# Attention's product written transposed to two column halves, copied, transposed back; its normalization later

## What is computed

```
x = layernorm(x + edge_layer(x, adj, adj, b))          # layer 0, "edge"
x = layernorm(x + graph_attention(x, W, a, beta, adj)) # layer 1, "att" and "gat"
x = layernorm(x + (adj @ x) @ weight + bias)           # layer 2, "gcn"
q, k, v = x @ Wq + bq, x @ Wk + bk, x @ Wv + bv        # layer 3, 8 heads of 64
scores = q @ k.T / 8 + (0 where adj else -1e9)
x = layernorm(x + softmax(scores) @ v)                 # the change is in softmax(scores) @ v
```

## Time and profile before

| | |
|---|---|
| median of 3 runs | 2856.92 us (2856.85 to 2857.3) |
| the profiled execution | 2855.93 us |
| its span, first to last instruction | 2854.1 us |
| busy: TensorE, its loads, VectorE, ScalarE, GpSimd | 97%, 88%, 75%, 57%, 53% |
| mean granted TensorE clock | 0.990 |

### The profile page before, as it was taken

How to read it: one execution, slowest core, us unless ns; L and a number is a source line. 1 busy time by engine, 2 the same in 40 slices (tenths; PEclk the granted TensorE clock), 3 DMA queues, 4 the chain that set the end, 5 groups by cost and what they waited for, 6 DMA issues and landing times.

```text
span 2854.1 us, 59257 instructions
## 1 busy us (share of the span) xinstructions
PE 2773.0 (97%) x18569; PEld 2514.3 (88%) x18569; DVE 2151.3 (75%) x6805; ACT 1631.1 (57%) x4616; POOL 1507.2 (53%) x1808
## 2 busy tenths in 40 slices
PE   4899999999999999999999999999999999999996
PEld 3799998999999999999999999899999999999986
DVE  7777777777777777777777777777777777777763
ACT  3455656655555556556555555655555555556553
POOL 6555555545545555555555555555555555555541
PEclk9999999999999999999999999999999999999997
DMA  3000000000000000000000000000000000000000
GB/s 119 16 20 27 30 18 26 29 18 26 28 20 26 26 22 26 26 22 26 26 22 26 26 22 26 20 27 26 18 26 29 18 26 29 18 26 29 9 16 23
DMA packets 41471, 74.06 MB, mean 26 GB/s; under 512 B 5584, under 2 KB 5712, under 8 KB 41424
## 3 DMA queue, kind: packets, MB, share of 16 engines
q1 hardware_dynamic: 41424, 73.49, 7.9%
HBM read 39.92 MB, written 33.55 MB: 26 GB/s over the span
## 4 chain that ended last, share of the span: by engine, by line
PE 96%; DVE 1%; issue 1%; ACT 1%; DMA 0%; POOL 0%; ACTq 0%; SPq 0%; POOLq 0%; DVEq 0%
PE rot L812 22%; PE rot L814 22%; PE rot L813 22%; PE rot L912 9%; PE rot L920 4%; PE rot L869 4%; PE score L812 2%; PE score L813 2%; PE score L814 2%; PE rot L961 2%; PE rot L889 2%; PE rot L893 2%; PE att_bank L942 0%; PE s_bank L877 0%; DMA probs<-in_L_gnn_W 0%
## 5 line engine op out<-in xcount | busy, mean ns | idle before, releaser
L337 POOL TENSOR_TENSOR ve<-mv,eps_col 128x1 f32<-128x1 f32 (+1 forms) x448 | 95.2, 212 | 679.6 <-DVE mv L609 351.2
L359 POOL TENSOR_TENSOR x2b<-x,bias 128x512 f32<-128x512 f32 x128 | 216.4, 1690 | 448.5 <-DVE x L657 448.5
L812 PE MATMUL rot<-w_hi,y_hi 128*128 128x512 f32 x1024 | 426.5, 417 | 5.4 <-DVE y_lo L649 4.6
L814 PE MATMUL rot<-w_hi,y_lo 128*128 128x512 f32 x1024 | 404.4, 395 | 0.0
L813 PE MATMUL rot<-w_lo,y_hi 128*128 128x512 f32 x1024 | 402.8, 393 | 0.0
L437 ACT ACTIVATE k_hi<-rot,kb_col 64x256 fp32r<-64x256 f32 x512 | 240.5, 470 | 271.6 <-PE rot L814 266.7
L551 ACT ACTIVATE probs<-score,sc_nmax 128x128 f32<-128x128 f32 x1024 | 357.8, 371 | 11.4 <-DVE sc_nmax L773 11.4
L599 DVE SCALAR_TENSOR_TENSOR k_lo<-rot,kb_col,k_hi 64x256 fp32r<-64x256 f32 x512 | 247.5, 483 | 93.3 <-ACT k_hi L437 87.7
L912 PEld LDWEIGHTS rot<-v_sb,probs_t 128*128 128x128 f32 x2048 | 241.5, 194 | 69.8 <-issue 58.5
L812 PE MATMUL rot<-xt_hi,wk_hi 128*128 128x256 f32 x1024 | 299.8, 293 | 0.0
L599 DVE SCALAR_TENSOR_TENSOR q_lo<-rot,qb_col,q_hi 128x256 fp32r<-128x256 f32 x256 | 112.1, 479 | 239.9 <-ACT q_hi L437 239.9
(11 more groups left out here) (122 smaller groups left out, 8383.2 us busy)
## 6 DMA issues: line engine op xcount, KB each, us to landing
x_in<-in_x SPq DMA_DIRECT2D x128, 256.0 KB, 2.6
out_x<-x SPq DMA_DIRECT2D x128, 256.0 KB, 2.1
probs<-in_L_gnn_W SPq DMA_DIRECT2D x1, 1024.0 KB, 7.6
v_sb<-in_L_gnn_weight SPq DMA_DIRECT2D x1, 1024.0 KB, 7.1
probs<-in_L_gnn_Wv SPq DMA_DIRECT2D x1, 1024.0 KB, 5.5
v_sb<-in_L_gnn_Wq SPq DMA_DIRECT2D x1, 1024.0 KB, 5.4
probs<-in_L_gnn_Wk SPq DMA_DIRECT2D x1, 1024.0 KB, 5.1
x<-in_L_gnn_a SPq DMA_DIRECT2D x1, 512.0 KB, 4.6
```

What stands on the lines that cost most here:

```text
L359: pool.tensor_tensor(x2b[:, :], x2[:, slot.buf(L_GCN, 2), :], bias2[:, :], ALU.add)\
L812: pe.matmul(outp, lh, rh, start=first, stop=False)
L814: return pe.matmul(outp, ll, rh, start=False, stop=last)
```

## The change

- TensorE: each product swaps its operands. The 64 columns of v are the stationary operand (128x64), the transposed probabilities are streamed (128 columns), and the result stands transposed: head 0 of a chunk in partitions 0 to 63 of rot[3], head 1 in partitions 64 to 127.
- VectorE: a new copy of rot[3] to a new tile `o_t`, ahead of y2_lo.
- TensorE: four new transposes of `o_t` back into rot[3], behind the edge product and ahead of the attention's transpose.
- VectorE: the scaling into `o_norm` moves from behind y2_lo to behind edge_s, and waits for the transposes.
- GpSimd: `x4_init` moves ahead of the addition of `o_norm`.

```diff
+        o_t = sb("o_t", [P, GROUP * CHUNKS * P])
...
@@ gpsimd @@
+                if slot.on(L_V):
+                    ... x4_init (as removed below)
                 if slot.on(L_PV):
...
                     pool.tensor_tensor(res, res, o_norm[:, :, :], ALU.add).then_inc(x4_done, 1)
-                if slot.on(L_V):
-
-                    slot.wait(pool, x3_done, L_V)
-                    stored = (slot.graph(L_V) - slot.part(L_V) - BUFS) * (16 // GROUP) + 16
-                    if not (isinstance(stored, int) and stored <= 0):
-                        pool.wait_ge(out_stored[slot.part(L_V)], stored)
-                    pool.tensor_tensor(x4[:, slot.buf(L_V, BUFS), :], x3[:, slot.buf(L_V, 2), :],
-                                       bv_row[:, :], ALU.add).then_inc(x4_init, 1)
@@ vector @@
+                if slot.on(L_PV):
+
+                    slot.wait(dve, pv_mm, L_PV)
+                    slot.wait(dve, ot_mm, L_PV, 1)
+                    dve.tensor_copy(o_t[:, :], rot[3][:, :]).then_inc(o_t_done, 1)
                 if slot.on(L_GCN):
                     slot.wait(dve, y2_hi_done, L_GCN)
                     dve.tensor_tensor(y2_lo[:, :], rot[2][:, :], y2_hi[:, :].bitcast(F32), ALU.subtract)\
                         .then_inc(y2_lo_done, 1)
-                if slot.on(L_PV):
-                    ... o_norm (it waits for pv_mm)
...
                     dve.tensor_scalar(edge_s[:, :], mv["0"][:, e2, 0:1], edge_c[:, 0:1], edge_c[:, 0:1],
                                       ALU.add, ALU.subtract).then_inc(edge_s_done, 1)
+                if slot.on(L_PV):
+
+                    slot.wait(dve, ot_mm, L_PV)
+                    slot.wait(dve, inv_done, L_PV)
+                    slot.wait(dve, x4_done, L_PV, 1)
+                    dve.tensor_tensor(o_norm[:, :, :].rearrange("p g (c d) -> p (g c) d", d=HEAD),
+                                      rot[3][:, :].rearrange("p (h d) -> p h d", d=HEAD),
+                                      sc_inv[:, :].unsqueeze(2).to_broadcast([P, CHUNKS * TILES, HEAD]),
+                                      ALU.mult).then_inc(o_norm_done, 1)
@@ tensor @@
                     for g in range(GROUP):
                         for c in range(CHUNKS):
-                            for h in range(2):
-                                at = ((g * CHUNKS + c) * 2 + h) * HEAD
+                            at = (g * CHUNKS + c) * P
+                            for h, rows in enumerate(HEAD_ROWS):
                                 col = (slot.part(L_PV) * CHUNKS + c) * P + h * HEAD
-                                ins = pe.matmul(rot[3][:, at:at + HEAD], probs_t[:, c, g * 2 + h, :],
-                                                v_sb[:, first + g, col:col + HEAD], start=True, stop=True)
+                                ins = pe.matmul(rot[3][rows, at:at + P], v_sb[:, first + g, col:col + HEAD],
+                                                probs_t[:, c, g * 2 + h, :], start=True, stop=True)
                     ins.then_inc(pv_mm, 1)
...
                         ins.then_inc(setup_mm, 1)
+                if slot.on(L_PV):
+
+                    slot.wait(pe, o_t_done, L_PV)
+                    for n in range(GROUP * CHUNKS):
+                        ins = pe.transpose(rot[3][:, n * P:(n + 1) * P], o_t[:, n * P:(n + 1) * P], ident[:, :])
+                    ins.then_inc(ot_mm, 1)
                 if slot.on(L_ATT):
```

More of the change, by code:

```diff
@@ L221, in graph_layers_kernel @@
         (s2_mm, q_mm, y1_mm, k_mm, pt0_mm, pt1_mm, att_t_mm, z1_mm, y2_mm, pv_mm, edge_mm, score_mm,
-         z2_mm, xt_mm, v_mm) = (sem(n) for n in (
+         z2_mm, xt_mm, v_mm, ot_mm) = (sem(n) for n in (
             "s2_mm", "q_mm", "y1_mm", "k_mm", "pt0_mm", "pt1_mm", "att_t_mm", "z1_mm", "y2_mm",
-            "pv_mm", "edge_mm", "score_mm", "z2_mm", "xt_mm", "v_mm"))
+            "pv_mm", "edge_mm", "score_mm", "z2_mm", "xt_mm", "v_mm", "ot_mm"))
         (z0_done, q_hi_done, y1_hi_done, att_exp, k_hi_done, pt0_done, att_t_done, e1_done,
@@ L231, in graph_layers_kernel @@
         (q_lo_done, lrelu_done, att_max_done, att_nmax_done, y1_lo_done, att_inv_done, att_n_done,
-         pt1_done, r1_done, y2_lo_done, o_norm_done, inv_done, edge_max_done, edge_c_done,
+         pt1_done, r1_done, y2_lo_done, o_t_done, o_norm_done, inv_done, edge_max_done, edge_c_done,
          edge_s_done, edge_b_done, score_nmax_done, x1_done, dots_done,
@@ L236, in graph_layers_kernel @@
             "att_inv_done", "att_n_done", "pt1_done", "r1_done", "y2_lo_done",
-            "o_norm_done", "inv_done", "edge_max_done", "edge_c_done", "edge_s_done", "edge_b_done",
+            "o_t_done", "o_norm_done", "inv_done", "edge_max_done", "edge_c_done", "edge_s_done", "edge_b_done",
             "score_nmax_done", "x1_done", "dots_done", "x2_done",
@@ L393, in emit @@
                         .then_inc(r1_sum_done, 1)
+                if slot.on(L_V):
+                    slot.wait(pool, x3_done, L_V)
+                    stored = (slot.graph(L_V) - slot.part(L_V) - BUFS) * (16 // GROUP) + 16
+                    if not (isinstance(stored, int) and stored <= 0):
+                        pool.wait_ge(out_stored[slot.part(L_V)], stored)
+                    pool.tensor_tensor(x4[:, slot.buf(L_V, BUFS), :], x3[:, slot.buf(L_V, 2), :],
+                                       bv_row[:, :], ALU.add).then_inc(x4_init, 1)
                 if slot.on(L_PV):
```

## The result

The changed kernel takes 2822.27 us (median of 4 runs, 2821.39 to 2822.43) against 2856.89 us beside it: 34.6 us less, a ratio of 0.9878 with the interval 0.9861 to 0.9895. I had forecast 2833: the direction and the mechanism held, and the gain was nearly half as large again as forecast.

What follows compares the result with a forecast made beforehand. TensorE, busy 97% of the span, was taken as the bound. -0.655 + 0.44 = -0.215 us per slot over 121 slots gave -26 us, +2 us for the ends: 2830 us of span, 2833 us measured time; range 2812 to 2938.

Steps and rivals of the forecast that it cites:

- The product: TensorE's L912: both array halves stream at once, 0.11 us per stream, starts spread over 0.88 us instead of 1.81.
- The border: Exit from L912 to full-width L920: last narrow matmul lasts 0.275 us instead of handing over after 0.11, 0.165 us more.
- The hole hides the entry: Ahead of L912 on TensorE: the array is empty anyway because of the 0.26 us hole, so entry costs nothing.
- The transposes: Four more on TensorE behind the edge product, 0.11 us each: +0.44 us per slot, hidden by nothing.
- The copy: VectorE, between r1 and y2_lo: 0.69 us, ends 0.42 us before the transposes want to start, costs nothing.
- o_norm and GpSimd's order: VectorE's later o_norm has 2.5 us of slack at its TensorE reader; GpSimd's x4_init stands 0.7 us; both cost nothing.
- The ends: Thin slots and the serial, half-clock end of the kernel: +2 us in all.
- Sum: Per full slot -0.655 + 0.44 = -0.215 us, over 121 slots -26 us.
- Serial halves: Rival at L912: the two halves take turns, product stays at 1.81 us; +75 us, 2932 us; chance 0.27.
- Partial overlap: Rival at L912: each instruction takes some 0.08 us; +0.075 us per slot, 2868 us; chance 0.14.
- Late copy: Rival: VectorE work ahead holds the copy over 0.3 us longer, TensorE waits, 12 us per 0.1 us; chance 0.06.
- Wins more: Rival at L912: a 128-column stream takes under 0.11 us, exit free, block 0.88 us; -57 us, 2800 us; chance 0.05.

Runs made afterwards that it cites:

- two-and-two by turns: Changed kernel with the head order changed within a graph, two products (four instructions) to the lower half, then two to the upper: 2826.26 us, ratio 0.9893.
- two runs of opposite sign: Changed kernel with the product of before, copy and transposes kept: 2918.33 us; changed kernel without the four transposes back: 2762.12 us; both give wrong results.
- the halves apart: Changed kernel with the loop over the two heads outermost, all eight lower-half instructions before the eight upper ones: 2877.14 us, ratio 1.0071.

## Why the prediction was right, point by point

- **The bound.** TensorE's chain carried the change in every run: slots changed by what its start distances changed. Right.
- **The product.** Forecast 0.88 us of starts, measured 0.82. That the halves stream at once and one instruction per half costs 0.11 us is right. The term was mis-sized because I let the second half start a turn late, in program order ("8 pairs of turns and one over"); the two halves start together (two starts by 0.01 us), and two-and-two by turns confirmed that program order does not hold the second half back.
- **The border.** Forecast 0.275 us from the last narrow start to L926, measured 0.20, and 0.04 more within L926. I had let L920 wait for the full printed duration of the last narrow matmul, and it does not. This, after the product, is the other mis-sized term: the emptying costs 0.09 and not 0.165. Together the block with its border is 1.06 us instead of 1.155. The Trainium skill, "TensorEngine Tiling (Array Packing)", Key Properties, has a drain at a change of tiling mode; the runs agree in kind, with 0.09 us in behind a matmul of 512 columns, 0.12 to 0.15 in behind a transpose, and 0.09 us out, each beyond a normal handover.
- **The hole hides the entry.** Right, and shown: once closed, 0.09 us of it stay.
- **The transposes.** 0.44 us forecast and measured; 51 and 52 us over the full slots by two runs of opposite sign, where 53 follow from 0.44. I had priced what they cost at the ends as part of +2 us; these two runs show 8 to 10 us there, set against what the swap gains at the ends.
- **The copy.** 0.69 us forecast, 0.68 measured, hidden; 0.42 us early forecast, 0.41 measured. The late copy would have cost as priced: 0.27 us per slot took the whole gain.
- **o_norm and GpSimd's order.** Nothing forecast, nothing measured. I had GpSimd wait 0.7 us for the stores in every second slot; the profile shows L401 right behind L393 in such a slot, so that detail is wrong, at no cost. I had counted the landing of both stores, and the code waits for the first alone. The trace of the changed kernel bears it out: the two stores of that slot land at 1322.32 and 1322.98 us, and L401 starts at 1322.55, between them.
- **The ends.** +2 us forecast, +3 measured.
- **Sum.** -0.215 us per slot forecast, -0.30 measured: the difference of 0.09 is the product's late half (0.06) and the border (0.075, less 0.04 in L926). Times 121 it makes 11 us, and 11 were missed.
- **The rivals.** Serial halves: refuted by the block, and made visible with the halves apart, where the first four instructions keep 0.11 us. Partial overlap: refuted (0.82 us of starts, some 0.055 us per instruction, where it had 0.08). Late copy: refuted in the changed kernel, as no wait for the copy shows. Wins more: refuted, because the load is now shorter (137 ns against 192) and an instruction in one half still takes 0.11 us; that the stream sets this pace fits, but no run streamed fewer columns through a half.

## What to carry to other kernels

When a float32 matmul streams 64 columns and loads 128, try to swap the operands and put the two halves of outputs on the two halves of the array: here the block went from 1.81 to 1.02 us, and the transposes back ate 0.44 of the 0.79. Count each change between narrow and wide as about 0.1 us (0.09 to 0.15 in these runs), and put it where TensorE stands anyway. Before such a rebuild, look what the hole ahead of the block waits for: moving one 0.5 us exponential in another engine's queue gave 39 us, more than the whole change did, and left only 12 us for the change to gain.

## What the runs showed of the hardware that I had not expected

By all these rows, matmuls in the two column halves don't start in program order: with eight of the lower half ahead in the program, the fifth and the sixth both start between 0.44 and 0.52 us, in a half whose own pace is 0.11, and two per 0.11 us follow. The Trainium skill, "TensorE: Matmul & The Clock Gate", Part 3, says that matmuls start and end strictly in program order; that doesn't fit these rows, and the measurement decides. My own description of the kernel before, that each engine executes its queue strictly in order, is wrong for these matmuls too. How far ahead the second half may run is only bounded: with eight instructions of the first half ahead of it, it began with the fifth start of the first, and with four ahead it was hardly held back. The trace has no label for the half, so this rests on the counts and durations of the starts.

A hole closed ahead of a block of load-paced matmuls gave back more than its length: 0.24 us of hole and 0.08 us of the block (1.81 to 1.73), where the first load then lay hidden too.
